# A deeper ring of gathered rows in the first and the third aggregation of a graph and feed-forward network

## What is computed

```python
edge_index = jnp.stack([src, dst])
x = x + L0_gnn(layernorm(x), edge_index, ...)        # two GIN layers
x = x + L0_ffn(layernorm(x)[None], ...)[0]           # slice attention, 8 heads, 64 slices
x = x + L1_gnn(layernorm(x), edge_index, ...)        # one GCN layer
x = x + L1_ffn(layernorm(x)[None], ...)[0]           # 8 experts, the best 2 of each node

# L0_gnn
h = (1 + eps1) * x + segment_sum(x[src], dst)        # first aggregation, 256 features
h = relu(relu(h @ W1a + b1a) @ W1b + b1b)
h = (1 + eps2) * h + segment_sum(h[src], dst)        # second aggregation, 512 features
out = relu(h @ W2a + b2a) @ W2b + b2b

# L1_gnn
msgs = (x @ W)[src] * (dinv[src] * dinv[dst])[:, None]
out = segment_sum(msgs, dst) + b                     # third aggregation, 256 features
```

## Time and profile before

| | us |
|---|---|
| median of 3 runs | 4542.7 |
| lowest and highest of them | 4540.22 and 4554.68 |
| profiled execution, its own time | 4555.01 |
| its span in the trace | 4553.2 |

### The profile page before, as it was taken

The page is one execution under the profiler, slowest core; times in us unless marked ns, Lnnn a source line. Parts: engine busy times, 40 slices in busy tenths (PEclk is TensorE's granted clock), DMA queues, the critical chain, the costliest instruction groups (busy, mean ns, idle before and its releaser), DMA issues. The chain is left out here.

```text
span 4553.2 us, 40537 instructions
## 1 busy us (share of the span) xinstructions
PE 3420.3 (75%) x12357; PEld 2262.4 (50%) x12359; DVE 1485.9 (33%) x5675; ACT 497.9 (11%) x1162; POOL 2790.0 (61%) x2814
## 2 busy tenths in 40 slices
PE   2388788777878899999999976566566655648996
PEld 2255454444453444444444455445444444438996
DVE  5121112212121443344433445233333343442221
ACT  4010000010110000000000002000000000003432
POOL 3666666666646666667666502666666666635664
PEclk7698888889899999999999987777777877879998
DMA  5333333443349666666666537334334433326887
GB/s 187 91 112 111 109 112 111 120 120 111 109 124 331 192 203 188 193 190 191 192 199 200 176 107 244 107 113 118 119 116 122 121 112 115 115 83 174 204 212 184
DMA packets 321342, 687.10 MB, mean 151 GB/s; under 512 B 58977, under 2 KB 148301, under 8 KB 320855
## 3 DMA queue, kind: packets, MB, share of 16 engines
q0 software_dynamic: 169712, 474.01, 37.8%
q10 hardware_dynamic: 86448, 110.35, 7.2%
q1 hardware_dynamic: 64970, 100.14, 6.7%
HBM read 592.43 MB, written 99.13 MB: 152 GB/s over the span
## 5 line engine op out<-in xcount | busy, mean ns | idle before, releaser
L280 POOL DMA_INDIRECT s_edge_rows<-table,w_src_idx x2538 | 2492.6, 982 | 1271.7 <-issue 716.2
L320 PE MATMUL s_psA<-s_edge_rows,s_onehot 128*128 128x257 f32 (+2 forms) x4932 | 1692.5, 487 | 200.1 <-DMA s_edge_rows<-table,w_src_idx 101.1
L320 PEld LDWEIGHTS s_psA<-s_edge_rows,s_onehot 128*128 128x128 f32 x4932 | 1015.0, 210 | 748.6 <-issue 622.6
L295 DVE TENSOR_SCALAR s_onehot<-w_iota_row,w_dst_l 128x128 f32<-128x128 bf16 x2466 | 531.6, 296 | 28.9 <-PEq L149 15.6
L1994 POOL DMA_INDIRECT acc_rows<-s_y,s_tnode x105 | 166.3, 1583 | 132.5 <-DVE s_y L2117 101.3
L330 PE MATMUL s_psA<-s_edge_rows,s_early 128*128 128x257 f32 (+2 forms) x648 | 224.0, 472 | 13.9 <-issue 11.9
L980 PE MATMUL s_psM<-s_w2a,s_hT 128*128 128x512 f32 x392 | 198.8, 655 | 18.3 <-ACT s_hT L880 11.3
L2142 PE MATMUL s_psU<-s_xT,s_w 128*128 128x128 f32 x1680 | 210.2, 279 | 0.0
L2142 PEld LDWEIGHTS s_psU<-s_xT,s_w 128*128 128x128 f32 x1680 | 201.4, 196 | 0.3 <-issue 0.3
L2152 PE MATMUL s_psD<-moe_w,s_hT 128*128 x840 | 199.5, 381 | 0.0
L974 PE MATMUL s_psM<-s_h1T,s_w1b 128*128 128x512 f32 (+2 forms) x448 | 186.5, 560 | 7.5 <-issue 6.2
(11 more groups left out here) (358 smaller groups left out, 2788.5 us busy)
## 6 DMA issues: line engine op xcount, KB each, us to landing
s_w<-in_L_ffn_W_dram SPq DMA_DIRECT2D x105, 512.0 KB
s_edge_rows<-table,w_src_idx POOLq DMA_INDIRECT x2538
s_swT<-swt_rows SPq DMA_DIRECT2D x12, 1024.0 KB
table<-s_trow ACTq DMA_DIRECT2D x11, 1024.0 KB
own_rows<-s_own ACTq DMA_DIRECT2D x11, 1024.0 KB
s_self_h<-own_rows ACTq DMA_DIRECT2D x11, 1024.0 KB
swt_rows<-s_swT ACTq DMA_DIRECT2D x11, 1024.0 KB
extra_rows<-w_zeros SPq DMA_DIRECT2D x7, 896.0 KB
```

Source lines behind the costliest of these rows:

```text
L280: pool.indirect_dma_start(self.rows[:, g % self.SLOTS, t, :], None, self.table, bass.IndirectOffsetOnAxis(ap=src_idx[:, at:at + 1], axis=0 ...
L295: last = nc.vector.tensor_scalar(into[:, t, :], iota_row[:, q * P:(q + 1) * P], dst_l[:, at + t:at + t + 1], None, ALU.is_equal)
L320: last = nc.tensor.matmul(banks[b % 2][:, 0:w], self.onehot[:, g % self.AHEAD, t, :], self.rows[:, g % self.SLOTS, t, col:col + w], start= ...
```

## The change

Two arguments differ. The ring of the first aggregation has 14 slots instead of the default 8, that of the third 16 instead of 6. The second keeps 6.

```diff
-            edges = Edges(S, table1, T1_W, ((0, D + 1),), FP32, GPB - 1)
+            edges = Edges(S, table1, T1_W, ((0, D + 1),), FP32, GPB - 1, slots=14)
...
-            edges = Edges(S, table3, D, ((0, D),), FP32, 1, slots=6)
+            edges = Edges(S, table3, D, ((0, D),), FP32, 1, slots=16)
```

## The result

| | before | changed |
|---|---|---|
| median of 4 runs each, us | 4544.4 | 4591.59 |
| lowest and highest | 4540.22 and 4554.68 | 4588.55 and 4596.03 |
| span of the profiled execution | 4553.2 | 4588.6 |

The changed kernel takes 1.0102 of the time before (95% interval 1.0085 to 1.0119): 47 us or 1.0% slower. The prediction had 4535 and a range up to 4588, with 0.28 for slower. It was wrong.

A forecast was written before the change was run, and what follows sets the result against it. The prediction took PE's counts, late while POOL gathers without a break and prompt when it stops, to bound the kernel. Terms of +7 and -15 us made -8, from a median of 4542.7 to 4535 us, range 4465 to 4588.

The forecast's parts named there:

- +7 and -15 us for the two stages: Sums of the predicted terms for the first and the third aggregation, together -8 us.
- A full ring moves at the speed of the one who empties it: Both stages: the ring is nearly always full, so PE's counts set POOL's pace at any depth; no size of its own.
- The middle term 0: Middle of both stages: POOL runs further ahead, then stops as often, at PE's 4.3 us a group; 0 us.
- First aggregation, start, +22.6: First aggregation's start: POOL's first stop comes 18 gathers later, so PE stands 22.6 us longer.
- Its give-back, -10.8: First aggregation, after its start: PE finds 13 groups landed instead of 7, its later waits for landed rows go; -10.8 us.
- the end, -5: First aggregation's end: PE does 6 groups more after POOL's last gather, without its disturbance; 0 to -5.4, taken as -5 us.
- Third aggregation, start, 0: Third aggregation's start: PE's spare products begin without a POOL stop, so 0 us; upper end 37.7 us.
- The stops that vanish, -4: Third aggregation: POOL's stops of 4.25 and 4.99 us fall away, gathers come earlier; 0 to -8.6, taken as -4 us.
- the end, -11: Third aggregation's end: PE does ten groups more without POOL, at most 1.7 us saved each; 0 to -17, taken as -11.
- A: Rival: the ring's stops were needed, both starts grow by the full deferred stops; +44 us, 4587; chance 0.27.
- B: Rival: the deeper ring speeds the middle too; -80 us, 4462, if a quarter of the stops goes; chance 0.28.
- C: Rival: nothing happens, late counts have nothing to do with POOL's stops; 4543; inside the likeliest case's 0.45.

The follow-up runs named there:

- f1_deep_again: The changed kernel (14 and 16 slots) once more, unaltered, on a late chip: 4560.57 us beside 4510.26 for the kernel before, ratio 1.0113.
- g4_before: The kernel before (8, 6 and 6 slots), unaltered, run for its own trace: one run, 4517.58 us.
- g3_open_late: Changed kernel's buffers, but POOL waits for the group 8 and 6 back until group 139, then 14 and 16 back: 4559.72 us, ratio 1.0117.
- f2_pause6: The changed kernel with a pause of POOL before every sixth group of the first and third aggregations: 4596.92 us, ratio 1.0187.
- h1_busy6: The kernel before with rings of 4, 6, 4 and a POOL fill of 3072 floats a partition before every sixth group, first and third aggregations: ratio 1.0081.
- e1_first14: The kernel before with 14 slots in the first aggregation only, on the prompt chip: 4091.58 us beside 4089.18, ratio 1.0002.

## Why the prediction was wrong, step by step

The prediction had +7 and -15 us for the two stages, and they measured +21 and +20. Of these 49 us, 42 are one term: the third aggregation's start, which I put at 0. The other 7 are what the smaller terms add up to.

**"A full ring moves at the speed of the one who empties it": the wrong foundation, with a right number on it.** The middle term 0 was right, 71 and 72 gathers in 100 us, and 58 and 57 stops of 145 and 142 us (before 54 and 59, 147 and 149 us, counted in the same way). That was luck as to its reason. The cover that I named, PE's own pace of 4.3 us a group, is not what holds POOL. With PE down to 40.55 us in 100, or with PE only 3 us behind the gathers (4 slots), POOL's pace is the same. It is POOL's pace, with its late counts, that is given, and added slots only let PE fall further behind.

**First aggregation, start, +22.6: right in kind, somewhat small.** The changed kernel's timeline, PE and then POOL:

```profile
115.21 0.70 PE L374 MATMUL s_psM<-s_spare_rows,s_spare_onehot 128*128 128x257 f32 x2
169.58 4.34 PE L320 MATMUL s_psA<-s_edge_rows,s_onehot 128*128 128x257 f32 x12 [53.67 <-issue]
...
162.99 0.95 POOL L280 DMA_INDIRECT s_edge_rows<-table,w_src_idx  x1 [3.15 <-remote]
172.92 1.00 POOL L280 DMA_INDIRECT s_edge_rows<-table,w_src_idx  x1 [6.46 <-PE s_psA L320]
```

PE's 29.23 us became 53.67, where some 52 was foreseen. POOL's first stop began at 159.8, where 157 was foreseen, and DVE got the count with the second stop, at 168.45. By the last product of the first super-block the stage was 29.4 us late (131.9 us from the first gather, before 102.5).

**Its give-back, -10.8, and the end, -5.** PE's waits for landed rows did fall, from 26.1 to 19.2 us, less than I took. PE's lateness went from 29.4 us to 22.7 at POOL's last gather: 6.7 us came back where I had 10.8. The end gave 1.7 us more where I had 5. Sum +21.0 where I had +7.

**Third aggregation, start, 0: the step that failed most.** The changed kernel's timeline there, PE and then POOL:

```profile
2850.57 1.22 PE L374 MATMUL s_psO<-s_spare_rows,s_spare_onehot 128*128 128x256 f32 x2 [14.87 <-issue]
...
2860.18 2.75 PE L320 MATMUL s_psA<-s_edge_rows,s_onehot 128*128 128x256 f32 x12
2909.05 0.69 PE L1870 MATMUL s_psT<-w_ident,s_agg 128*128 128x128 f32 x2 [46.11 <-DVE s_agg L1767]
...
2908.81 0.95 POOL L280 DMA_INDIRECT s_edge_rows<-table,w_src_idx  x1 [5.88 <-remote]
```

The spare products came without a stop, as the earlier trace rows had suggested. I ended the step with them. But 12 us later PE needs the next count, DVE's sum of block 0, and that one did wait for POOL's first stop: 46.11 us. The waits of PE for DVE in the earlier trace rows were the nearest row for it, and they were named in my first part. By the end of the first super-block the stage was 42 us late (145.4 against 103.4), more than the 37.7 of my upper end.

**The stops that vanish, -4, and the end, -11: about right.** POOL's stops fell by 7 us in all, and its time by 9. PE's lateness went from 42.0 us to 36.8 at POOL's last gather, and in the ten groups more that it does behind it, to 20.3. Sum +20.3 where I had -15, and the whole of the difference is the start.

The terms beside what they measured, as PE's lateness at the same product, counted from the stage's first gather. The last column is the repetition, f1_deep_again against g4_before:

| | predicted | measured | repeated |
|---|---|---|---|
| first: start, to the end of the first super-block | +22.6 | +29.4 | +28.2 |
| its give-back, to POOL's last gather | -10.8 | -6.7 | -2.4 |
| its end | -5 | -1.7 | -6.7 |
| third: start, to the end of the first super-block | 0 | +42.0 | +46.6 |
| stops that vanish, to POOL's last gather | -4 | -5.2 | -3.7 |
| its end | -11 | -16.5 | -14.7 |

**What the sum lacked.** If POOL's pace stays as it is and the ring is full, PE must be six and ten groups further behind in the middle: at 4.3 us a group that is an estimate of 26 and 43 us. It measured 23 and 38 us (means of blocks 8 to 40; repeated 26 and 42). The prediction let PE be only 11.8 and 0 us late and still let POOL's pace and the full ring stand; both cannot hold. This also says why a shorter wait at the start saves nothing. Behind POOL's last gather PE then has six and ten groups more to do than before, at 20.0 us (3.3 each) and 29.7 us (3.0 each).

**The rivals.** Of what I put down, A came nearest: its 4587, the starts at +22.6 and +37.7 less the ends, is 5 us off. Its mechanism is half of the truth: g3_open_late has the same loss with the starts of before, so it is the ring's filling up and not the stage's start. B is excluded by the middle, C by the interval.

**The range.** The upper end, 4588, was A's own sum rounded up, so A had no room above it. A's ends, -16, were right (-18.2). Its two starts were 11 us too small, and it left out the 12 us that came back, so that its +44 fits the stages' +41 partly by luck.

## What to carry to other kernels

A deeper buffer between two engines can only help the one that waits for it. So ask first whose pace will stay as it is, and whether the engine that fills the buffer will be through sooner. If not, the added depth is worked off behind it, at the consumer's price for each entry, and the smallest ring that keeps the pace is the best one (here 4 groups).

When a step is put off, follow all counts that are waited for in the time by which it is put off, not only the first. And before an effect of a few per cent is built on a stop that nothing in the program explains, see whether it is there on another chip.

## What was not expected of the hardware

- The same kernel takes 4089 us on one chip and 4510 to 4544 on others, at equal gathers (953 ns, a new one every 1.26 us). POOL's time for 846 gathers is 1071 to 1077 us on the one and 1203 to 1230 on the others, 1131 and 1253 to 1276 in the second aggregation at 6 slots, whose rows are twice as wide. So the surcharge goes by the gather and not by the bytes: 0.15 to 0.18 us each. (Pauses and fills left aside.)
- The sum of breaks is nearly fixed, not the breaks. Stops of 3 us, pauses of 1.8, fills of 2.7 and fills of 0.19 us behind every gather all count for the most part into it: 130 to 149 us of stops without pauses or fills, 145 to 158 together with those of f2_pause6 and h1_busy6.
- On the late chips counts between engines were late by some 10 us: POOL went on 9 to 13 us (medians) after the end of the product that it waited for, at 4 to 16 slots. The prediction set this against the 26 ns of the Trainium skill, "TensorE: Matmul & The Clock Gate", section "The cost: per-tile semaphore tail". On the prompt chip DVE's 49 waits at line 924 (444.4 us) are all ended by a product or by DVE's own work in the records, while on the first result's chip 288.5 us of 526.3 have no recorded event, here of the kernel before's first aggregation and that of e1_first14:

```profile
L924 DVE TENSOR_TENSOR w_degree<-w_degree,s_psA 128x1 f32<-128x1 f32 x49 | 7.5, 153 | 526.3 <-remote 288.5 <-PE s_psA L320 132.3 <-PE s_psA L330 67.9
```
```profile
L924 DVE TENSOR_TENSOR w_degree<-w_degree,s_psA 128x1 f32<-128x1 f32 x49 | 7.4, 152 | 444.4 <-PE s_psA L330 432.5 <-PE s_psA L320 11.7 <-DVE x_xl L911 0.2
```
